# The sort of a graph kernel's edges: a 16-bit select whose sum lies in PSUM, a later release of GpSimd's spread, and fewer, longer relus on ScalarE

## Chip, cores and metric

One core of a Trainium2 chip. The metric is the device time of one execution in microseconds (us), lower is better.

## What is computed

A graph of N = 12,500 nodes with 64 features each and E = 412,500 directed edges (`src`, `dst`) with 4 attributes per edge passes two layers:

```
h = relu(layernorm(x));  x = x + L0(h, edges)      # hyperbolic attention layer: gather, edge weight, segment sum by source
h = relu(layernorm(x));  x = x + L1(h, edges, attr)  # message passing: gather, two products with batch norm, segment sum, two more
```

Both layers gather rows by the edge's two ends and sum over the edges of one source node. For both the kernel first sorts the edges by the chunk of 128 nodes to which their source belongs. The change lies in this sort alone, and the sort computes nothing but an order: each edge becomes a record (source within its chunk, destination, 4 attributes) in a table `rec_d`, where the records of one chunk stand together.

## The kernel before, in words

The program is written out by hand as phases with a barrier of all engines between them: a first norm and product, the sort (its supertiles run from about 315 us to about 2,880 us), the gathers and sums of the two layers, and the node updates. Within a phase every engine has its own instruction list in program order, and the engines hold each other by semaphores. There are no queues or planners that reorder anything.

The sort runs over NS = 124 supertiles. One supertile has J = 26 edges in each of 128 partitions (3,328 edges). NC = 99 is the number of chunks with a spare one. What one supertile s needs, engine by engine (lines are those of the kernel before):

- **VectorE, `flags` (L619):** one 0/1 row of 99 for each edge, equal to 1 at its chunk, in bfloat16 (`B3`, 2,574 elements for each partition, two buffers). It is done one supertile ahead, inside `supertile(s-1)`.
- **TensorE, `ranks` (L736 to L742):** 65 products with these rows (13 + 13 + 13 + 26) give the counts by chunk in PSUM (`RT`). At the end it signals `rt_rdy`.
- **VectorE, `supertile` (L654 to L697):** waits for `rt_rdy`; turns counts into starts (`INC`, L657), adds both (`A2`, two rows of 99, in PSUM, L658); selects for each of the 26 edges its own entry of `A2` by a product with the flags (L664, into `prod`, 2,574 float32) and a sum over 99 (L668, into `sel`); then a few operations on 26 elements split the position into a segment and a place in it (L669 to L675); L679 makes a one-hot of the place (`OHL`). After `seg_rdy` ScalarE may start. Then come the flags of s+1 (L619), 10 of the 26 segment one-hots of 512 columns (L686, `DH`), `before` for s+1 (L627 to L633), and the destinations (L691 to L697).
- **ScalarE, `segments` (L786, L792):** the other ACTD = 16 one-hots, as relu(1 - (iota - segment)^2): 16 squares, then 16 relus in place, each over one segment of 512, and at the end `da_rdy`.
- **GpSimd, `spread` (L835, L837):** multiplies the edges' 15 values by `OHL`, 624 and 2,496 elements, into `EX`. It reads `OHL` of s, but waits for `l_rdy`, which VectorE gives inside `supertile(s+1)`, between L658 and L664. At its end it gives `e_rdy`. Ahead of it stand `attributes` (L818 to L827), behind it four indirect DMAs (`scatter`, L849) for s-1.
- **TensorE, `place` (L752, L754):** waits for `e_rdy`, `d_rdy` and `da_rdy`; four passes of 27 products put the values into the places. At the end it gives `y_rdy`. TensorE's loop is `place(s)`, then `ranks(s+2)`.
- **VectorE, `take_out` (L641 to L645):** the last part of `supertile(s+1)` waits for `y_rdy` and copies the result of s out of PSUM.

So the release of the spread of s and the counts that `supertile(s+2)` starts with are tied together by TensorE's order:

```
    place(b)      # waits for e_rdy of s: the spread, released by l_rdy inside supertile(s+1)
    ranks(b)      # gives rt_rdy, for which supertile(s+2) waits at L654
```

Of the kernel before, what the change touches and what calls it, by code (L numbers as in the profile page):

```python
# [8 lines left out]
BF16 = mybir.dt.bfloat16  # L9
I32 = mybir.dt.int32  # L10
U16 = mybir.dt.uint16
ALU = mybir.AluOpType
ACT = mybir.ActivationFunctionType
AX = mybir.AxisListType.X
# [2 lines left out]
P = 128  # L17
# [32 lines left out]
def build(nc, x, src, dst, attr, w0t, wm1, bm1, gm1, betm1, wm2, bm2, gm2, betm2,  # L50
# [14 lines left out]
    with ctx:  # L65
# [341 lines left out]
        late_at = top[0]  # L407
        EX = [take(J * CH * L // 2, BF16) for _ in range(2)]
        EX4 = [e.rearrange("p (j c l) -> p j c l", c=CH, l=L) for e in EX]
        JNC = J * NC // 2  # L410
        B = [HA[:, 3 * COLS + b * JNC:3 * COLS + (b + 1) * JNC].bitcast(BF16) for b in range(2)]
        assert 3 * COLS + 2 * JNC <= NC * (D + AGW)
        B3 = [x.rearrange("p (j c) -> p j c", c=NC) for x in B]
        prod = take(J * NC)
        late_end = top[0]
        attb = [take(J * 4) for _ in range(2)]
        rem = take(J * 4)
# [4 lines left out]
        earlier_f = take(GJ * GJ)  # L422
        earlier = take(GJ * GJ // 2 + 1, BF16)[:, 0:GJ * GJ]
        wp = [take(J) for _ in range(2)]
        sel, seg_f = take(J), [take(J) for _ in range(2)]
        q_i, sg_i, l_i = (take(J, I32) for _ in range(3))
        stage = [take(NW * L * REC) for _ in range(2)]
        stage4 = [z.rearrange("p (w l c) -> p w l c", l=L, c=REC) for z in stage]
        ix = [take(NW, I32) for _ in range(2)]
        ACTD = 16  # L430
        iota_w = take(WS // 2, BF16)
        crow = take(NW * CH * L // 2, BF16)
        crow4 = crow.rearrange("p (w c l) -> p w c l", c=CH, l=L)
# [38 lines left out]
        RT = [ps[:, b * 512:b * 512 + 384] for b in range(2)]  # L472
        Y = [ps[:, 1024 + b * 512:1024 + b * 512 + NW * CH * L] for b in range(2)]
        Y4 = [y.rearrange("p (w c l) -> p w c l", c=CH, l=L) for y in Y]
        A2 = ps[:, 2048:2048 + 2 * NC].rearrange("p (g c) -> p g c", g=2)
        l_f = ps[:, 2560:2560 + J]
        zps = ps[:, 2560 + J:2561 + J].to_broadcast([P, NC])

        s_v, s_cntd, s_mm, s_pool, s_ld, s_bl, s_clr, h_rdy, h_used, s_hist, s_cast = (
# [12 lines left out]
        with nc.Block() as block:  # L492
# [37 lines left out]
            def _(v):  # L530
# [50 lines left out]
                for c, value in enumerate((-1.0, float(N // P * P), float(N % P))):  # L581
                    v.memset(crow4[0:1, :, c, :], value)
                v.memset(ANC[:, 0:1], 0.0)
                v.memset(ps[:, 2560 + J:2561 + J], 0.0)
                v.memset(ANC[:, NC + 1:NC + 2], float(DUMP + MID))
                link(v.memset(INC[:, 0:1], float(-MID)))
# [22 lines left out]
                def need(n):  # L609
                    v.wait_ge(s_c, n)  # L610
# [5 lines left out]

                def flags(b, s):

                    n = go(v.tensor_tensor(B3[b], iota_b[:, 0:NC].unsqueeze(1).to_broadcast([P, J, NC]),  # L619
                                           S[:, ds(s * J, J)].unsqueeze(2).to_broadcast([P, J, NC]), ALU.is_equal))  # L620
                    need(n)
                    v.sem_inc(b_rdy, 1)

# [27 lines left out]
                def supertile(b, s, first=False, last=False):  # L651
                    consume(v, rt_rdy)
                    n_all = RT[b][:, 256:256 + NC]
                    need(go(v.tensor_scalar(n_i, n_all, float(L - 1), None, ALU.add)))  # L654
                    need(go(v.tensor_scalar(n_i, n_i, 3, 3, ALU.logical_shift_right, ALU.logical_shift_left)))
                    need(go(v.tensor_copy(n8, n_i)))
                    need(go(v.tensor_tensor_scan(INC[:, 1:NC + 1], n8, zps, float(-MID), ALU.add, ALU.add)))  # L657
                    a2 = go(v.tensor_tensor(A2, INC[:, 0:NC].unsqueeze(1).to_broadcast([P, 2, NC]),  # L658
                                            RT[b][:, 0:256].rearrange("p (g c) -> p g c", g=2)[:, :, 0:NC], ALU.add))
                    go(v.tensor_tensor(gpos[1 - b], gpos[b], n_all, ALU.add))  # L660
                    need(a2)
                    if not first:
                        v.sem_inc(l_rdy, 1)
                    n = go(v.tensor_tensor(prod.rearrange("p (g j c) -> p g j c", g=2, j=GJ),  # L664
                                           B[b].rearrange("p (g j c) -> p g j c", g=2, j=GJ),
                                           A2.unsqueeze(2).to_broadcast([P, 2, GJ, NC]), ALU.mult))
                    need(n)
                    need(go(v.tensor_reduce(sel, prod.rearrange("p (j c) -> p j c", c=NC), AX, ALU.add)))  # L668
                    need(go(v.tensor_tensor(q_i, sel, wp[b], ALU.add)))  # L669
                    sg = go(v.tensor_scalar(sg_i, q_i, 3, None, ALU.arith_shift_right))  # L670
                    li = go(v.tensor_scalar(l_i, q_i, L - 1, None, ALU.bitwise_and))
                    need(sg)
                    seg = go(v.tensor_copy(seg_f[b], sg_i))
                    need(li)
                    lf = go(v.tensor_copy(l_f, l_i))  # L675
                    need(seg)
                    v.sem_inc(seg_rdy, 1)
                    need(lf)
                    need(go(v.tensor_tensor(OHL[b], iota_b[:, 0:L].unsqueeze(1).to_broadcast([P, J, L]),  # L679
                                            l_f.unsqueeze(2).to_broadcast([P, J, L]), ALU.is_equal)))  # L680
                    if not last:
                        flags(1 - b, s + 1)
                    if first:
                        v.wait_ge(s_cast, 5)
                    for j in range(J - ACTD):
                        n = go(v.tensor_scalar(DH[b][:, j * WS:(j + 1) * WS], iota_w, seg_f[b][:, j:j + 1], None, ALU.is_equal))  # L686
                    need(n)
                    v.sem_inc(d_rdy, 1)
                    if not last:
                        before(1 - b, s + 1)  # L690
                    need(go(v.tensor_tensor(ANC[:, 1:NC + 1], gpos[b], INC[:, 0:NC], ALU.subtract)))  # L691
                    need(go(v.tensor_tensor(STEP, ANC[:, 1:NC + 2], ANC[:, 0:NC + 1], ALU.subtract)))
                    for w in range(NW):
                        n = go(v.scalar_tensor_tensor(out=hit3[:, w, :], in0=INC, scalar=g8[:, w:w + 1], in1=STEP,
                                                      op0=ALU.is_le, op1=ALU.mult, accum_out=dsum[:, w:w + 1]))
                    need(n)
                    go(v.tensor_tensor(dest[b], dsum, g8, ALU.add))  # L697
                    if not first:
                        take_out(1 - b)
                    settle()  # L700
# [17 lines left out]
            def _(t):  # L718
# [14 lines left out]
                def ranks(b):  # L733
                    consume(t, b_rdy)
                    for j in range(GJ):
                        t.matmul(RT[b][:, 0:NC], tri_b, B3[b][:, j, :], start=(j == 0), stop=(j == GJ - 1))  # L736
                    for j in range(GJ, J):
                        t.matmul(RT[b][:, 128:128 + NC], tri_b, B3[b][:, j, :], start=(j == GJ), stop=False)
                    for j in range(GJ):
                        t.matmul(RT[b][:, 128:128 + NC], ones_b, B3[b][:, j, :], start=False, stop=(j == GJ - 1))  # L740
                    for j in range(J):
                        m = t.matmul(RT[b][:, 256:256 + NC], ones_b, B3[b][:, j, :], start=(j == 0), stop=(j == J - 1))  # L742
                    m.then_inc(rt_rdy, 1)

                def place(b):
# [21 lines left out]
            @block.scalar  # L767
            def _(a):
                a.wait_ge(s_v, 1)
                a.activation(Hd, I0, ACT.Copy).then_inc(s_cast, 1)  # L770
                a.wait_ge(s_v, 4)
                a.activation(S, I0, ACT.Copy).then_inc(s_cast, 1)
                a.wait_ge(s_hist, 1)
                a.wait_ge(s_v, 8)
                a.activation(PC[:, :, 0], I0, ACT.Copy, bias=1.0).then_inc(s_cast, 1)
                a.activation(PC[:, :, 1], I1, ACT.Copy, scale=-1.0).then_inc(s_cast, 1)
                a.activation(PC[:, :, 2], s_i, ACT.Copy, scale=-1.0).then_inc(s_cast, 1)

                a.wait_ge(s_cast, 5)

                def segments(b):
                    consume(a, seg_rdy)
                    consume(a, da_free[b])
                    for n in range(ACTD):
                        j = J - ACTD + n
                        a.activation(DH[b][:, j * WS:(j + 1) * WS], iota_w, ACT.Square, scale=-1.0,  # L786
                                     bias=seg_f[b][:, j:j + 1]).then_inc(s_sq, 1)
                    for n in range(ACTD):
                        j = J - ACTD + n
                        a.wait_ge(s_sq, n + 1)  # L790
                        o = DH[b][:, j * WS:(j + 1) * WS]
                        last = a.activation(o, o, ACT.Relu, scale=-1.0, bias=1.0)  # L792
                    last.then_inc(da_rdy, 1)
                    a.sem_inc(s_sq, -ACTD)
                with a.Fori(0, NS // 2) as i:
                    for b in range(2):
                        segments(b)
# [1476 lines left out]
```

## Time and profile before

| | |
|---|---|
| runs shown | 14502.01 us median of 3 (14497.61 to 14504.36) |
| the profiled execution's own time | 14510.89 us, its span 14509.2 us |
| sort, steady part: starts of L664 in the last 120 supertiles | 404.6 to 2837.8 us |
| busy over the span | PE 6055.6, VectorE 8188.4, ScalarE 4342.2, GpSimd 9916.9 us |

The busy times are sums over phases of quite different kinds: in the slices of the sort VectorE and ScalarE are busy nearly all the time, in the gather phases GpSimd alone is. Since the change touches the sort only, its stretch is what is to be read, and there one period from a supertile to the next. In a timeline, the number in brackets is the engine's idle time just before the row and what ended it; `DVEq`, `POOLq` and `ACTq` are the engines' own sequencers, which is how a wait on a semaphore shows.

### The profile page before, as it was taken

To read this page: it belongs to the slowest core of one execution; us is meant where nothing else is said; L and a number is where in the kernel's file an instruction comes from. 1 tells how busy PE (TensorE), PEld (TensorE's weight loads), DVE (VectorE), ACT (ScalarE), POOL (GpSimd) and SP (SyncE) were. 2 spreads that over 40 slices of the span, in tenths; PEclk is the share of its full clock that TensorE was granted. 3 is DMA by queue.
4 is the path that set the end of the run, shared out by engine and by line. 5 is a ranking of instruction groups with operands and counts; after the bars stand their busy time and mean duration, and the time that the engine had idled before them with its cause. 6 is when DMAs were issued, how large, how long until landed. Compare 5 with 4: busy or idle time off the path is not lost. (4 is left out here: it accounts for less than half of the span.)

```text
span 14509.2 us, 190139 instructions
## 1 busy us (share of the span) xinstructions
PE 6055.6 (42%) x50077; PEld 5002.8 (34%) x50078; DVE 8188.4 (56%) x17598; ACT 4342.2 (30%) x8364; POOL 9916.9 (68%) x10589
## 2 busy tenths in 40 slices
PE   3555555511111111111179633333333333388998
PEld 3554555511111111101178522222222222236997
DVE  6999999743343334334388844444444444467776
ACT  1888888800000000000078500000000000054334
POOL 0666666677777777777767467777777777704774
PEclk6777777755555555555599866666666666699999
DMA  2000000033333333333344322222222222274332
GB/s 68 9 9 9 9 9 9 17 92 88 88 87 88 88 88 86 88 84 91 81 129 151 93 77 81 81 81 81 81 81 82 81 81 81 79 249 132 106 106 77
DMA packets 1142542, 1160.65 MB, mean 80 GB/s; under 512 B 688977, under 2 KB 832977, under 8 KB 1142226
## 3 DMA queue, kind: packets, MB, share of 16 engines
q1 hardware_dynamic: 845842, 680.39, 16.7%
q0 software_dynamic: 235008, 248.13, 8.6%
q10 hardware_dynamic: 61632, 231.44, 4.1%
q8 instruction: 24, 0.39, 0.0%
q14 instruction: 36, 0.29, 0.0%
HBM read 872.56 MB, written 286.75 MB: 80 GB/s over the span
## 5 line engine op out<-in xcount | busy, mean ns | idle before, releaser
L1611 POOL DMA_INDIRECT big<-b_d,big x3424 | 3276.2, 957 | 1223.1 <-issue 978.0
L1097 POOL DMA_INDIRECT big<-h_d,big x3424 | 3308.0, 966 | 1054.6 <-issue 989.9
L1151 PE MATMUL ps<-big 128*128 x3424 | 653.3, 371 | 3687.2 <-PEq L148 3685.0
L1151 PEld LDWEIGHTS ps<-big 128*128 128x128 bf16 x3424 | 500.8, 164 | 3839.5 <-issue 3839.5
L1685 PE MATMUL ps<-big 128*128 x3424 | 566.3, 317 | 2845.9 <-PEq L148 2845.9
L1182 DVE TENSOR_TENSOR HA<-big 128x1024 f32<-128x1024 f32 x214 | 262.2, 1225 | 2559.4 <-DVEq L148 2558.4
L1685 PEld LDWEIGHTS ps<-big 128*128 128x128 bf16 x3424 | 410.1, 156 | 3164.8 <-issue 3164.7
L1934 POOL TENSOR_SCALAR big<-iota_f,big 128x128 f32<-128x128 f32 x1498 | 877.7, 609 | 814.5 <-DMA big<-rec_d 499.7
L1724 DVE TENSOR_TENSOR big<-ps,big 128x1024 f32<-128x1024 f32 x214 | 262.1, 1225 | 2057.6 <-DVEq L148 2057.6
L786 ACT ACTIVATE big<-big 128x512 bf16<-128x512 bf16 x1984 | 1228.9, 708 | 280.7 <-ACTq L148 280.7
L1105 ACT ACTIVATE big<-big 128x16 int32<-128x16 f32 x214 | 49.3, 230 | 4203.2 <-ACTq L148 4179.1
L792 ACT ACTIVATE big<-big 128x512 bf16<-128x512 bf16 x1984 | 1042.3, 614 | 0.0
L849 POOL DMA_INDIRECT rec_d<-big x496 | 839.3, 1692 | 282.1 <-POOLq L148 154.0
L1620 ACT ACTIVATE big<-big 128x16 int32<-128x16 f32 x214 | 49.1, 229 | 3104.5 <-ACTq L148 3104.5
L754 PE MATMUL ps<-big 128*128 128x120 bf16 x12896 | 976.5, 252 | 0.0
L754 PEld LDWEIGHTS ps<-big 128*128 128x128 bf16 x12896 | 952.1, 119 | 0.0
L1317 POOL TENSOR_SCALAR big<-iota_f,big 128x128 f32<-128x128 f32 x856 | 687.1, 818 | 265.4 <-DMA big<-rec_d 233.5
L1392 PE MATMUL ps<-big 128*128 128x128 f32 x6848 | 816.3, 277 | 102.2 <-DVE big L1317 89.3
L1392 PEld LDWEIGHTS ps<-big 128*128 128x128 f32 x6848 | 783.1, 192 | 135.2 <-issue 133.3
L1728 DVE TENSOR_REDUCE ps<-ps 128x256 f32<-128x768 f32 x856 | 820.5, 959 | 0.0
L2010 PE MATMUL ps<-big 128*128 128x64 f32 x6848 | 788.4, 273 | 1.0 <-DVE big L1934 0.9
L2010 PEld LDWEIGHTS ps<-big 128*128 128x128 f32 x6848 | 781.9, 192 | 1.2 <-issue 1.2
(407 smaller groups left out, 14633.5 us busy)
## 6 DMA issues: line engine op xcount, KB each, us to landing
big<-e_d SPq DMA_DIRECT2D x428, 512.0 KB, 3.2
rows_d<-big ACTq DMA_DIRECT2D x214, 544.0 KB, 2.8
big<-rows_d SPq DMA_DIRECT2D x214, 544.0 KB, 3.3
HA<-slots_d SPq DMA_DIRECT2D x214, 512.0 KB
big<-slots_d SPq DMA_DIRECT2D x214, 512.0 KB
e_d<-big ACTq DMA_DIRECT2D x214, 512.0 KB
big<-rec_d SPq DMA_DIRECT2D x860, 64.0 KB, 3.0
big<-h_d,big POOLq DMA_INDIRECT x3424
```

The source lines that it names most:

```text
L754: m = t.matmul(o, DH[b][:, j * WS + w * P:j * WS + (w + 1) * P], EX[b][:, j * CH * L:(j + 1) * CH * L], start=False, stop=(j == J - 1))
L786: a.activation(DH[b][:, j * WS:(j + 1) * WS], iota_w, ACT.Square, scale=-1.0, bias=seg_f[b][:, j:j + 1]).then_inc(s_sq, 1)
L792: last = a.activation(o, o, ACT.Relu, scale=-1.0, bias=1.0)
L849: gp.indirect_dma_start(rec_d, bass.IndirectOffsetOnAxis(ix[b][:, w:w + 1], 0), stage[b][:, w * L * REC:(w + 1) * L * REC], None).then_inc ...
L1097: gp.indirect_dma_start(G[g][:, t * ROW:(t + 1) * ROW], None, h0_d, bass.IndirectOffsetOnAxis(idx[g][:, t:t + 1], 0)).then_inc(gath[g], 16)
L1151: m = t.matmul(XS[h][:, n, 0:3 * D + 3], OT3[g % 2][:, o, :], T0[:, ds(chunks[o // 2] * TW, 3 * D + 3)], start=True, stop=True)
L1392: m = t.matmul(ps[:, o:o + P], O4[g][:, n * P:(n + 1) * P], G0[g][:, n * ROW:n * ROW + P], start=(n % 2 == 0), stop=(n % 2 == 1))
L1611: gp.indirect_dma_start(G[g][:, t * D:(t + 1) * D], None, b_d, bass.IndirectOffsetOnAxis(idx[g % 2][:, t:t + 1], 0)).then_inc(gath[g], 16)
L1685: m = t.matmul(XST[q % 2][:, n // 2, n % 2, :], OT3[g % 2][:, o, :], T1[:, ds(chunks[o // 2] * (3 * D), 3 * D)], start=True, stop=True)
L1728: v.tensor_reduce(x, XSQ[q % 2], AX, ALU.add).then_inc(s_e, 1)
L1934: last = eng.tensor_scalar(u1.O[b][:, n * P:(n + 1) * P], iota_f[:, :], u1.rec[b][:, n * REC:n * REC + 1], None, ALU.is_equal)
L2010: m = t.matmul(ps[:, o:o + D], u1.O[b][:, n * P:(n + 1) * P], MSG[b][:, n * D:(n + 1) * D], start=(n % 2 == 0), stop=(n % 2 == 1))
```

## The change

1. The chunk rows are one column longer, NCP = NC + 1 = 100 (`flags` writes 2,600 elements; the products in `ranks` still read 99 of each 100).
2. `A2` moves from PSUM to SBUF and is int16; `prod` is int16 too. So the select's product (L664) has two inputs in SBUF, all of 2 bytes.
3. A new addition folds the second 50 columns of `prod` onto the first 50 (1,300 elements, in place), and the reduce (L668) runs over 50 columns for each edge.
4. Its sum `sel` is in PSUM, no longer in SBUF.
5. `l_rdy` is given behind the new addition, no longer ahead of the product.
6. ACTD is 17: ScalarE makes 17 of the 26 one-hots, VectorE 9. The 17 relus become two, over 9 and 8 segments.

```diff
-        JNC = J * NC // 2
+        NCP = NC + 1
+        assert NCP % 4 == 0
+        JNC = J * NCP // 2
-        prod = take(J * NC)
+        prod = take(J * NCP // 2, I16)
+        prod3 = prod.rearrange("p (j c) -> p j c", c=NCP)
+        take(J * NC - J * NCP // 2)
-        sel, seg_f = take(J), [take(J) for _ in range(2)]
+        seg_f = [take(J) for _ in range(2)]
-        ACTD = 16
+        ACTD = 17
+        HALF = (ACTD + 1) // 2
-        A2 = ps[:, 2048:2048 + 2 * NC].rearrange("p (g c) -> p g c", g=2)
+        A2f = take(NCP, I16)
+        A2 = A2f.rearrange("p (g c) -> p g c", g=2)
+        sel = ps[:, 2624:2624 + J]
...
                     need(a2)
+                    n = go(v.tensor_tensor(prod.rearrange("p (g j c) -> p g j c", g=2, j=GJ),
+                                           B[b].rearrange("p (g j c) -> p g j c", g=2, j=GJ),
+                                           A2.unsqueeze(2).to_broadcast([P, 2, GJ, NCP]), ALU.mult))
+                    need(n)
+                    need(go(v.tensor_tensor(prod3[:, :, 0:NCP // 2], prod3[:, :, 0:NCP // 2],
+                                            prod3[:, :, NCP // 2:NCP], ALU.add)))
                     if not first:
                         v.sem_inc(l_rdy, 1)
-                    n = go(v.tensor_tensor(prod.rearrange("p (g j c) -> p g j c", g=2, j=GJ),
-                                           B[b].rearrange("p (g j c) -> p g j c", g=2, j=GJ),
-                                           A2.unsqueeze(2).to_broadcast([P, 2, GJ, NC]), ALU.mult))
-                    need(n)
-                    need(go(v.tensor_reduce(sel, prod.rearrange("p (j c) -> p j c", c=NC), AX, ALU.add)))
+                    need(go(v.tensor_reduce(sel, prod3[:, :, 0:NCP // 2], AX, ALU.add)))
...
-                    for n in range(ACTD):
-                        j = J - ACTD + n
-                        a.wait_ge(s_sq, n + 1)
-                        o = DH[b][:, j * WS:(j + 1) * WS]
+                    for n, m in ((0, HALF), (HALF, ACTD)):
+                        a.wait_ge(s_sq, m)
+                        o = DH[b][:, (J - ACTD + n) * WS:(J - ACTD + m) * WS]
                         last = a.activation(o, o, ACT.Relu, scale=-1.0, bias=1.0)
```

VectorE inside `supertile(s+1)`, from the sum `A2` to the first segment one-hot. Before:

```order
L658 TENSOR_TENSOR ps<-big,ps 128x198 [waits so_chain]
L660 TENSOR_TENSOR big<-big,ps 128x99
L664 TENSOR_TENSOR big<-HA,ps 128x2574 [waits so_chain]
L668 TENSOR_REDUCE big<-big 128x26 [waits so_chain]
L669 TENSOR_TENSOR big<-big 128x26 [waits so_chain]
L670 TENSOR_SCALAR big<-big 128x26 [waits so_chain]
L671 TENSOR_SCALAR big<-big 128x26
L673 CAST big<-big 128x26 [waits so_chain]
L675 CAST ps<-big 128x26 [waits so_chain]
L679 TENSOR_TENSOR big<-iota_b,ps 128x208 [waits so_chain]
L619 TENSOR_TENSOR HA<-iota_b,HA 128x2574 [waits so_chain]
```

Of the change (its line numbers are higher by 9 to 11):

```order
L667 TENSOR_TENSOR big<-big,ps 128x2x99 [waits so_chain]
L669 TENSOR_TENSOR big<-big,ps 128x99
L671 TENSOR_TENSOR big<-HA,big 128x2600 [waits so_chain]
L675 TENSOR_TENSOR big<-big 128x26x50 [waits so_chain]
L679 TENSOR_REDUCE ps<-big 128x26 [waits so_chain]
L680 TENSOR_TENSOR big<-ps,big 128x26 [waits so_chain]
L681 TENSOR_SCALAR big<-big 128x26 [waits so_chain]
L682 TENSOR_SCALAR big<-big 128x26
L684 CAST big<-big 128x26 [waits so_chain]
L686 CAST ps<-big 128x26 [waits so_chain]
L690 TENSOR_TENSOR big<-iota_b,ps 128x208 [waits so_chain]
L628 TENSOR_TENSOR HA<-iota_b,HA 128x2600 [waits so_chain]
```

One operation has come in between the product and the reduce (L675 of the changed kernel). `l_rdy` is given behind it, where it was given ahead of the product. The reduce now writes PSUM, and the operation behind it reads PSUM.

ScalarE's part of one supertile, in the changed kernel:

```order
L797 ACTIVATE big<-big 128x512 [waits so_seg,so_dafree1]
L797 ACTIVATE big<-big 128x512 x16
L802 ACTIVATE big<-big 128x4608 [waits so_square]
L802 ACTIVATE big<-big 128x4096 [waits so_square]
```

Two relus stand where 16 were, and there are 17 squares (L797).

## Rows read from the trace of the kernel before

**Rows 1.** Line L664 as a source, 400 to 2850 us: duration min/median/max, first and last start
```profile
L664 DVE TENSOR_TENSOR big<-HA,ps x120: 2835/2835/2837, 404.6 to 2837.8; 128x2574 f32<-128x2574 bf16 x120
```

**Rows 2.** Who waited for whom, 400 to 2850 us: total us, times, longest us
```profile
ACT big L786 <- ACTq L148: 267.3, 120, 2.4
```

**Rows 3.** Timeline of one supertile: start us, us, engine, line, operation, [idle before]
```profile
1999.89 2.84 DVE L664 TENSOR_TENSOR big<-HA,ps 128x2574 f32<-128x2574 bf16 x1
2000.18 1.24 POOL L835 TENSOR_TENSOR big<-HA,big 128x624 bf16<-128x624 bf16 x1 [3.89 <-POOLq L148]
2001.38 4.40 POOL L837 TENSOR_TENSOR big<-big 128x2496 bf16<-128x2496 bf16 x1
...
2005.86 0.18 DVE L670 TENSOR_SCALAR big<-big 128x26 int32<-128x26 int32 x1
...
2006.33 0.11 PEld L752 LDWEIGHTS ps<-big 128*128 128x128 bf16 x1 [9.89 <-issue]
...
2006.95 2.84 DVE L619 TENSOR_TENSOR HA<-iota_b,HA 128x2574 bf16<-128x2574 bf16 x1 [0.18 <-DVE big L679]
2007.01 3.69 POOL L849 DMA_INDIRECT rec_d<-big  x1 [1.23 <-POOLq L148]
...
2012.60 1.53 PE L754 MATMUL ps<-big 128*128 128x120 bf16 x26
...
2015.77 1.37 PE L742 MATMUL ps<-HA,big 128*128 128x99 bf16 x26
...
2018.50 0.26 DVE L654 TENSOR_SCALAR big<-ps 128x99 int32<-128x99 f32 x1 [0.46 <-DVEq L148]
...
2020.20 2.83 DVE L664 TENSOR_TENSOR big<-HA,ps 128x2574 f32<-128x2574 bf16 x1
```

**Rows 4.** Stretches: length, busy us (and count) by engine, PEclk granted, DMA share, GB/s
```profile
2006.40:2008.40 2.00, 2.00 (x21) 2.00 (x22) 1.82 (x2) 1.88 (x4) 1.39 (x1) 0.50 0.00 0
...
2012.60:2017.10 4.50, 4.50 (x95) 4.38 (x91) 4.02 (x16) 4.50 (x9) 3.63 (x7) 1.00 0.07 19
```

**Rows 5.** Groups of the sort by line: total us, mean ns
```profile
L786 ACT ACTIVATE big<-big 128x512 bf16<-128x512 bf16 x1984 | 1228.9, 708 | 280.7 <-ACTq L148 280.7
L792 ACT ACTIVATE big<-big 128x512 bf16<-128x512 bf16 x1984 | 1042.3, 614 | 0.0
...
L686 DVE TENSOR_SCALAR big<-big 128x512 bf16<-128x512 bf16 x1240 | 416.1, 406 | 18.9 <-DVE HA L619 9.3
...
L668 DVE TENSOR_REDUCE big<-big 128x26 f32<-128x2574 f32 x124 | 351.3, 2833 | 4.3
...
L633 DVE TENSOR_REDUCE big<-big 128x26 f32<-128x338 bf16 x124 | 62.7, 505 | 4.3
L627 DVE TENSOR_TENSOR big<-HA 128x338 bf16 x120 | 61.3, 511 | 18.0 <-DVE big L686 9.0
...
L631 DVE TENSOR_TENSOR big<-big 128x338 bf16<-128x338 bf16 x124 | 41.7, 336 | 4.3
...
L655 DVE TENSOR_SCALAR big<-big 128x99 int32<-128x99 int32 x124 | 26.3, 212 | 4.4
...
L670 DVE TENSOR_SCALAR big<-big 128x26 int32<-128x26 int32 x124 | 22.1, 178 | 4.3
```

**Rows 6.** Timeline of the second supertile, where VectorE and GpSimd meet
```profile
349.84 0.27 POOL L818 CAST big<-big 128x104 bf16<-128x104 f32 x1 [0.34 <-POOLq L148]
349.88 0.26 DVE L673 CAST big<-big 128x26 f32<-128x26 int32 x1
...
350.69 2.84 DVE L619 TENSOR_TENSOR HA<-iota_b,HA 128x2574 bf16<-128x2574 bf16 x1
350.73 2.93 POOL L823 CAST big<-big 128x104 bf16<-128x104 f32 x1 [0.17 <-POOL big L820]
```

**Rows 7.** Timeline of the first supertile: the end of the ranks, VectorE's next
```profile
321.67 2.37 PE L742 MATMUL ps<-HA,big 128*128 128x99 bf16 x26
...
324.19 0.26 DVE L654 TENSOR_SCALAR big<-ps 128x99 int32<-128x99 f32 x1 [4.36 <-DVEq L148]
```

More of the change, by code:

```diff
@@ L11 @@
 U16 = mybir.dt.uint16
+I16 = mybir.dt.int16
 ALU = mybir.AluOpType
@@ L409, in build @@
         EX4 = [e.rearrange("p (j c l) -> p j c l", c=CH, l=L) for e in EX]
-        JNC = J * NC // 2
+        NCP = NC + 1
+        assert NCP % 4 == 0
+        JNC = J * NCP // 2
         B = [HA[:, 3 * COLS + b * JNC:3 * COLS + (b + 1) * JNC].bitcast(BF16) for b in range(2)]
         assert 3 * COLS + 2 * JNC <= NC * (D + AGW)
-        B3 = [x.rearrange("p (j c) -> p j c", c=NC) for x in B]
-        prod = take(J * NC)
+        B3 = [x.rearrange("p (j c) -> p j c", c=NCP) for x in B]
+        prod = take(J * NCP // 2, I16)
+        prod3 = prod.rearrange("p (j c) -> p j c", c=NCP)
+        take(J * NC - J * NCP // 2)
         late_end = top[0]
@@ L583, in _ @@
                 v.memset(ANC[:, 0:1], 0.0)
+                v.memset(A2f, 0.0)
                 v.memset(ps[:, 2560 + J:2561 + J], 0.0)
@@ L617, in flags @@
                 def flags(b, s):
-                    n = go(v.tensor_tensor(B3[b], iota_b[:, 0:NC].unsqueeze(1).to_broadcast([P, J, NC]),
-                                           S[:, ds(s * J, J)].unsqueeze(2).to_broadcast([P, J, NC]), ALU.is_equal))
+                    n = go(v.tensor_tensor(B3[b], iota_b[:, 0:NCP].unsqueeze(1).to_broadcast([P, J, NCP]),
+                                           S[:, ds(s * J, J)].unsqueeze(2).to_broadcast([P, J, NCP]), ALU.is_equal))
                     need(n)
@@ L657, in supertile @@
                     need(go(v.tensor_tensor_scan(INC[:, 1:NC + 1], n8, zps, float(-MID), ALU.add, ALU.add)))
-                    a2 = go(v.tensor_tensor(A2, INC[:, 0:NC].unsqueeze(1).to_broadcast([P, 2, NC]),
+                    a2 = go(v.tensor_tensor(A2[:, :, 0:NC], INC[:, 0:NC].unsqueeze(1).to_broadcast([P, 2, NC]),
                                             RT[b][:, 0:256].rearrange("p (g c) -> p g c", g=2)[:, :, 0:NC], ALU.add))
@@ L735, in ranks @@
                     for j in range(GJ):
-                        t.matmul(RT[b][:, 0:NC], tri_b, B3[b][:, j, :], start=(j == 0), stop=(j == GJ - 1))
+                        t.matmul(RT[b][:, 0:NC], tri_b, B3[b][:, j, 0:NC], start=(j == 0), stop=(j == GJ - 1))
                     for j in range(GJ, J):
-                        t.matmul(RT[b][:, 128:128 + NC], tri_b, B3[b][:, j, :], start=(j == GJ), stop=False)
+                        t.matmul(RT[b][:, 128:128 + NC], tri_b, B3[b][:, j, 0:NC], start=(j == GJ), stop=False)
                     for j in range(GJ):
-                        t.matmul(RT[b][:, 128:128 + NC], ones_b, B3[b][:, j, :], start=False, stop=(j == GJ - 1))
+                        t.matmul(RT[b][:, 128:128 + NC], ones_b, B3[b][:, j, 0:NC], start=False, stop=(j == GJ - 1))
                     for j in range(J):
-                        m = t.matmul(RT[b][:, 256:256 + NC], ones_b, B3[b][:, j, :], start=(j == 0), stop=(j == J - 1))
+                        m = t.matmul(RT[b][:, 256:256 + NC], ones_b, B3[b][:, j, 0:NC], start=(j == 0), stop=(j == J - 1))
                     m.then_inc(rt_rdy, 1)
```

## Prediction

> **What bounds the kernel now.** The change lies in the sort alone, so I read one period of the sort, not the page's shares. First the product L664 as a source: between its first and last start lie 119 supertiles, (2837.8 - 404.6) / 119 = **20.45 us a period** [rows 1]. Then who waits: ScalarE stands before its squares for 267.3 / 120 = 2.2 us a supertile [rows 2]. In the timeline of one supertile GpSimd stood idle for 3.89 us before its spread, TensorE for 9.89 us before its placement, VectorE for only 0.46 us before L654 [rows 3], mostly the handling of semaphores. So VectorE sets the period.
>
> The timeline [rows 3] shows a second loop that doesn't bind yet. The spread starts 0.29 us after L664 does, when `l_rdy` is given (1999.89 to 2000.18), and lasts 5.60 us (to 2001.38 + 4.40 = 2005.78). The placement starts 0.55 us later (2006.33), and placement and the ranks behind it end at 2015.77 + 1.37 = 2017.14, which is 10.81 us. Only then can the supertile after next pass L654. In the first supertile, where VectorE really waited, L654 came 0.15 us after the last rank (321.67 + 2.37 = 324.04 to 324.19) [rows 7]. From L654 to L664 are 1.70 us. Sum: 0.29 + 5.60 + 0.55 + 10.81 + 0.15 + 1.70 = 19.10 us from one L664 to the next. Against 20.45 that is a slack of 1.35 us, **and the change puts its new delay of `l_rdy` into this loop**.
>
> **The change, part by part.**
>
> *The select.* L631 and L627 both have 338 elements of 2 bytes; L631 (a product, in place) takes 336 ns, L627 (one input repeats each element) 511 [rows 5]. L668 and L633, reduces of 2,574 and 338 elements, give (2833 - 505) / 2236 = 1.04 ns an element and 153 ns fixed. So L627 runs at one element a step, 1.04 ns, L631 at two, 0.52 ns with 160 ns fixed. The new product has 2-byte operands that run along rows of 100 as L631's do: 2,600 x 0.52 + 160 = 1.51 us in place of 2.84. The new addition: 1,300 x 0.52 + 160 = 0.84 us. The reduce, 1,300 elements: 1,300 x 1.04 + 153 = 1.51 us in place of 2.83. With a step of 0.03 us behind each of the first two, `l_rdy` comes at 2.42 us after the product's start, where it came at 0. No row has a product of bfloat16 with int16. Its bounds are L631's rate (1.51 us) and L664's own (2.84 us at 2,574 elements, 2.87 at 2,600); I take the first, since L631 is nearest in width and layout. The operands in PSUM (`sel`, its reader) change operations of 26 elements, bounded by their 0.2 us rows: nothing.
>
> *VectorE's own sum.* Before, L664 to L670 took 2005.86 - 1999.89 = 5.97 us [rows 3]. Now the same way is 2.42 + 1.51 + 0.03 for the reduce, 0.24 for the operation behind it = 4.20 us, 1.77 less. One one-hot fewer: L686 has a mean of 0.41 us, ten of them overlapped in about 3.4, so 0.34 less. The flags have 26 elements more: 0.03 us. If nothing else held VectorE, its period would be 20.45 - 2.08 = 18.37 us.
>
> *ScalarE.* 16 squares keep it busy for 1228.9 / 124 = 9.91 us, 16 relus for 1042.3 / 124 = 8.41 [rows 5]. 17 squares: 10.53 us. The relus over 17 segments cost 8.93 us at most, at the old price by segment, less with two long ones; the engine thus needs no more than 19.5 us. Under a period of over 21 us this is hidden in either case; it would cost something only if the period came under 19.5.
>
> *The release.* The loop above grows by 2.42: 19.10 + 2.42 = **21.52 us**. That alone is 1.07 us above today's period. The spread gets no shorter by the change, nor do placement and ranks (99 columns each as before).
>
> *What the spread now meets on VectorE.* This is the larger term. Two pairs of rows [rows 6] show that the engines hold each other. VectorE's L619 (two inputs in SBUF) ran from 350.69 to 353.53; a GpSimd cast that began at 350.73 and should take 0.27 us took 2.93, till 353.66. And it goes the other way too: GpSimd's L818 held 349.84 to 350.11, VectorE's L673 began at 349.88 and ended at 350.14, 0.26 us in place of 0.18. GpSimd's L849, which began 0.06 us after L619, needed 3.69 us [rows 3]. Before the change the spread (2000.18 to 2005.78) lay beside L664 and L668 alone, which have one input in SBUF each, and both engines ran undisturbed; it ended 0.08 us before L670. Now it starts at 2.42 + 0.29 = 2.71 us behind the product's start and ends at 8.31, while VectorE comes to L670 at 4.20. L670 is one of the kind of L673: 26 elements of 4 bytes, SBUF to SBUF. L655 and L670, the same operation on 99 and 26 elements, take 212 and 178 ns [rows 5], 0.47 ns an element, half of 1.04, so this kind reads two elements a step and can be expected to need what GpSimd holds. L837 takes over from L835 at 3.91, before L670 is there. I take it that L670 waits for the end of L837, as L673 did for L818; the nearest row is that one, with a wait of hundredths. Its start is then as if at 8.31 + 0.10 - 0.18 = 8.23 us, where it was at 5.97: **2.26 us later**. Less 0.34, plus 0.03, the period is 20.45 + 1.95 = **22.40 us**. The bounds: no wait at all, and the loop of 21.52 us binds; a wait as taken, 22.40.
>
> The Trainium skill says in "SBUF — State Buffer", section "Who interferes with whom", that a VectorE instruction in a mode with two ports, or with two SBUF inputs while GpSimd reads SBUF, and a GpSimd instruction exclude each other for the whole instruction, and that whoever issues first wins. By that rule L670 waits to the end of L837, 4.1 us, which is the 22.40; without it the sum would be 21.52. The 2.93 us of L823 agree with it; that VectorE stands behind a GpSimd instruction of 4.4 us no row here shows.
>
> *The wait that VectorE then carries.* Behind L670 stand its signal to ScalarE, the flags, the one-hots and `take_out`. ScalarE gets its segments at about 8.9 us in place of 6.6; it ends 18 to 19.5 us later, at 28.4 at most, while their placement starts at 22.40 + 8.86 = 31.3. Covered. The first scatter DMA still starts 1.23 us after the spread, beside the flags, which still begin about 1.1 us after it, so that meeting stays as it is. The ranks end at 8.86 + 10.81 = 19.67 and L654 is due at 22.40 - 1.70 = 20.70: the second loop has 0.9 us to spare.
>
> *Sum.* About 122 of the 124 supertiles run so (the first has no release; the second is not yet in step). 122 x 1.95 = 238 us. The profiled execution took 14510.89 us, so 14749; it stands 8.9 above the median of 14502, so **14740**. The rest of the program isn't touched.
>
> **The rivals.**
>
> *No wait at L670, or only at the flags* (17%). Short operations may not be held, and L619, which has two inputs in SBUF and would be due at 5.3, then waits until 8.31. From L619 to the next L664 are 2020.20 - 2006.95 = 13.25 us [rows 3], 12.94 with one one-hot fewer, so VectorE's loop is 21.3 us and the one through TensorE binds at 21.52: 122 x 1.07 = 131 us, **14633**. For it: the held rows are few. Against it: L673's stretched row.
>
> *The product runs at one element a step* (8%), since its types are mixed. Then `l_rdy` comes 1.36 us later still, and both loops with it: 122 x 3.31 = 404 us, **14905**. For it: no row has such a product. Against: all three tensors are 2 bytes wide.
>
> *The scatter gets ahead of the flags* (5%): the first L849 and L619 are due within 0.2 us of each other. Before, L849 had 3.69 - (2006.95 + 2.84 - 2007.01) = 0.91 us left when L619 was through, its own work. If it comes first and holds VectorE for these 0.91 us, the period is that much longer: 14740 + 122 x 0.91 = **14851**.
>
> *Faster* (7%): TensorE leaves the lower of its clock levels earlier, and L670 isn't held. The placement starts at a granted clock of 0.50, 1.2 GHz, after 9.89 us of idleness, and its last pass and the ranks run at 1.00, 2.4 GHz [rows 4]. From the placement's start to its last pass are 2012.60 - 2006.33 = 6.27 us; at that pass's pace [rows 3] 3 x 1.53 = 4.59, 1.68 less. The loop would be 19.84 us, 0.61 under today's: **14428**. It decides from where placement and ranks together fall from 10.81 below 9.74 us. Against it: TensorE's idle time gets longer with the period, and it has to start each placement from idleness as before. VectorE's 18.37 us alone, 122 x 2.08 = 254 us gained (14248), can't be reached while the spread's loop stands.
>
> *No change* (3%): the same mechanism, half way.
>
> **How the numbers follow.** The likeliest case, L670 held, has 60%: 14740. A measurement of this kernel tells about 0.2%, 29 us, from no change. Slower by more than that are all cases but the last two: 60 + 17 + 8 + 5 = 90%; within it 3%; faster 7%. The range leaves out the product at one element a step and the faster cases, 18%: from 14620, a little under the loop of 21.52 us, to 14855, above the scatter's case.
>
> **What the changed profile would show.** The period of the select's product 22.4 us; the product near 1.51, the addition 0.84, the reduce 1.51 us; the first operation on 26 int32 elements at 4.2 us mean in place of 0.18, ending with GpSimd's L837; L837 still at 4.40; GpSimd's scatter unchanged; ScalarE's wait before the squares up from 2.2 to about 4 us. The forecast is wrong if that operation stays at 0.18 us: then the flags are stretched or L654 waits for TensorE, and the period is 21.5. A product of 2.87 us would be the second rival. A period under 20.4 needs placement and ranks under 9.7 us.

## The result and the profile after

The changed kernel takes 14728.56 us (median of 4, 14727.46 to 14735.67), the kernel before 14502.05 us in the same comparison: ratio 1.0158, 95% interval 1.0145 to 1.0171. It is slower by 226.5 us, where 238 were forecast (14740, range 14620 to 14855).

The select's product as a source, in the profile of the changed kernel, answers to [rows 1]:

```profile
L671 DVE TENSOR_TENSOR big<-HA,big x120: 1502/1504/1507, 405.3 to 3059.5; 128x2600 int16<-128x2600 bf16 x120
```

(3059.5 - 405.3) / 119 = **22.30 us a period**, where it was 20.45, so 1.86 us more; 22.40 was forecast. 226.5 / 1.86 = 122 supertiles, so the whole loss lies here. The product takes 1504 ns, as forecast (1.51 us): bfloat16 times int16 runs at two elements a step like L631.

The waits of the steady part; ScalarE's answers to [rows 2]:

```profile
POOL big L845 <- POOLq L149: 714.5, 117, 6.4
ACT big L797 <- ACTq L149: 503.9, 116, 4.6
...
DVE big L663 <- DVEq L149: 74.0, 117, 0.8
```

ScalarE stands 503.9 / 116 = 4.3 us before its squares (2.2 before), GpSimd 6.1 us before its spread. VectorE stands 74.0 / 117 = 0.6 us at L663, which waits for the ranks, and stood 0.6 us at the same place before (75.0 us in 120 times at L654): the loop through TensorE doesn't bind.

The timeline of one supertile, which answers to [rows 3]:

```profile
2011.55 1.50 DVE L671 TENSOR_TENSOR big<-HA,big 128x2600 int16<-128x2600 bf16 x1
2013.09 0.84 DVE L675 TENSOR_TENSOR big<-big 128x1300 int16<-128x1300 int16 x1
2014.07 1.51 DVE L679 TENSOR_REDUCE ps<-big 128x26 f32<-128x1300 int16 x1
2014.37 1.24 POOL L845 TENSOR_TENSOR big<-HA,big 128x624 bf16<-128x624 bf16 x1 [6.34 <-POOLq L149]
2015.57 4.40 POOL L847 TENSOR_TENSOR big<-big 128x2496 bf16<-128x2496 bf16 x1
2015.62 0.18 DVE L680 TENSOR_TENSOR big<-ps,big 128x26 int32<-128x26 f32 x1
2015.84 4.16 DVE L681 TENSOR_SCALAR big<-big 128x26 int32<-128x26 int32 x1
2019.92 0.17 DVE L682 TENSOR_SCALAR big<-big 128x26 int32<-128x26 int32 x1
...
2020.51 0.10 PEld L763 LDWEIGHTS ps<-big 128*128 128x128 bf16 x1 [11.48 <-issue]
...
2020.92 2.87 DVE L628 TENSOR_TENSOR HA<-iota_b,HA 128x2600 bf16<-128x2600 bf16 x1 [0.18 <-DVE big L690]
2021.19 3.50 POOL L859 DMA_INDIRECT rec_d<-big  x1 [1.23 <-POOLq L149]
...
2023.94 2.91 DVE L697 TENSOR_SCALAR big<-big 128x512 bf16<-128x512 bf16 x9 [0.16 <-DVE HA L628]
...
2030.91 7.54 ACT L802 ACTIVATE big<-big 128x4608 bf16<-128x4608 bf16 x2
...
2032.08 0.26 DVE L663 TENSOR_SCALAR big<-ps 128x99 int32<-128x99 f32 x1 [0.47 <-DVEq L149]
...
2033.71 1.50 DVE L671 TENSOR_TENSOR big<-HA,big 128x2600 int16<-128x2600 bf16 x1
```

The product begins at 2011.55, the addition takes 0.84 us, and release and reduce come at 2014.07; GpSimd's spread begins 0.30 us later and ends at 2015.57 + 4.40 = 2019.97. The first shift on 26 elements, L681, has 0.18 us of work; it begins at 2015.84 and ends at 2020.00. Two other signs stand in the same lines: L847 kept its 4.40 us, so it was VectorE that waited, and the next operation, L682, is back at 0.17 us. The flags (L628) begin 0.92 us after the end of L681, and the DMA instruction L859, which starts beside them, takes 3.50 us, where it took 3.69. The wait is no accident of one supertile; L681 as a source, min/median/max:

```profile
L681 DVE TENSOR_SCALAR big<-big x120: 4158/4161/4169, 409.6 to 3063.8; 128x26 int32<-128x26 int32 x120
```

The groups of the sort on ScalarE, and VectorE's one-hots, against [rows 5]:

```profile
L797 ACT ACTIVATE big<-big 128x512 bf16<-128x512 bf16 x2108 | 1304.7, 707 | 537.8 <-ACTq L149 537.8
...
L802 ACT ACTIVATE big<-big 128x4608 bf16<-128x4608 bf16 x124 | 499.4, 4028 | 0.0
L802 ACT ACTIVATE big<-big 128x4096 bf16<-128x4096 bf16 x124 | 446.5, 3601 | 0.0
L697 DVE TENSOR_SCALAR big<-big 128x512 bf16<-128x512 bf16 x1116 | 359.8, 393 | 18.9 <-DVE HA L628 9.3
```

The two relus take 4.03 and 3.60 us where 16 took 8.41; 17 squares and two relus are 10.53 + 7.53 = 18.1 us, which is hidden.

### The profile page after: what moved, and what is told of

Same layout as the page of the kernel before. It is cut to its first block and busy times, and to the rows that moved or that the text cites. A ratio compares the mean times of both kernels' runs of the same rounds, so it can differ in the third digit from the quotient of the medians.

```text
span 14734.0 us, 188528 instructions
## 1 busy us (share of the span) xinstructions
PE 6030.3 (41%) x50077; PEld 4977.4 (34%) x50078; DVE 8398.2 (57%) x17599; ACT 4310.2 (29%) x6752; POOL 9847.4 (67%) x10589
## 5 line engine op out<-in xcount | busy, mean ns | idle before, releaser
L797 ACT ACTIVATE big<-big 128x512 bf16<-128x512 bf16 x2108 | 1304.7, 707 | 537.8 <-ACTq L149 537.8
L859 POOL DMA_INDIRECT rec_d<-big x496 | 779.9, 1572 | 283.4 <-POOLq L149 155.1
L802 ACT ACTIVATE big<-big 128x4608 bf16<-128x4608 bf16 x248 | 934.2, 3814 | 0.0
```

What stands on the lines that cost most here:

```text
L859: gp.indirect_dma_start(rec_d, bass.IndirectOffsetOnAxis(ix[b][:, w:w + 1], 0), stage[b][:, w * L * REC:(w + 1) * L * REC], None).then_inc ...
```

## The experiments

**Take the small operations off GpSimd's path** (`x1_small_in_psum`). Positions, segments and places move to PSUM, so no shift or cast goes from SBUF to SBUF:

```diff
-        q_i, sg_i, l_i = (take(J, I32) for _ in range(3))
+        take(3 * J)
+        q_i, sg_i, l_i = (ps[:, 2688 + n * 32:2688 + n * 32 + J].bitcast(I32) for n in range(3))
```

> The changed kernel with q_i, sg_i and l_i in PSUM, so that the shifts and casts on 26 elements no longer go from SBUF to SBUF. Theory A (these operations need what GpSimd holds during its spread, and the wait of 4.16 us at the first of them sets the period of 22.31 us): they take about 0.2 us again, the flags, which have two inputs in SBUF, are then the ones that wait, till the spread's end; VectorE's loop falls to 21.3 us and the loop through the spread, placement and ranks binds at 21.5: 14728 - 122 x 0.8 = about 14630 us. Theory B (the wait only fills a gap; the late release alone, through TensorE, costs the time): no change, 14728.

Measured: 14654.74 us (ratio to before 1.0102, 1.0085 to 1.0119). Its product as a source gives (2979.0 - 406.0) / 119 = 21.62 us a period:

```profile
L672 DVE TENSOR_TENSOR big<-HA,big x120: 1502/1505/1508, 406.0 to 2979.0; 128x2600 int16<-128x2600 bf16 x120
```

Its timeline, GpSimd's second multiplication, the first shift, the flags:

```profile
2010.06 4.40 POOL L848 TENSOR_TENSOR big<-big 128x2496 bf16<-128x2496 bf16 x1
...
2010.33 0.19 DVE L682 TENSOR_SCALAR ps<-ps 128x26 int32<-128x26 int32 x1
...
2011.45 5.72 DVE L629 TENSOR_TENSOR HA<-iota_b,HA 128x2600 bf16<-128x2600 bf16 x1 [0.18 <-DVE big L691]
```

The shift takes 0.19 us beside the running spread. The flags, with two inputs in SBUF, begin at 2011.45 and end at 2017.17, 5.72 us for 2.87 us of work: they started while L848 ran and got through 2.7 us after its end at 2014.46. So theory A holds in both halves, and B, by which nothing would change, falls. A wait of 4.0 us is gone and one of 2.85 has come in its place. The stretched flags aren't alone in setting this period: in 78 of 117 supertiles of the steady part L664 starts less than 0.2 us after the last rank, so it waited for TensorE; in the change that is so in 11 of 117.

**Take the flags off it as well** (`x2_flags_too`):

```diff
+        iota_q = ps[:, 2944:2944 + NCP]
+                v.tensor_copy(iota_q, iota_f[:, 0:NCP])
-                    n = go(v.tensor_tensor(B3[b], iota_b[:, 0:NCP].unsqueeze(1).to_broadcast([P, J, NCP]),
+                    n = go(v.tensor_tensor(B3[b], iota_q.unsqueeze(1).to_broadcast([P, J, NCP]),
```

> As x1, and the flags read their row of numbers from PSUM, so nothing on VectorE meets the spread. Theory A with the second loop (spread, placement and ranks come behind the release, and the supertile after next waits for the ranks): VectorE would need 18.4 us a period, but now waits for TensorE at the first operation of the supertile, about 3 us each; period 21.5, about 14630 us, the same as x1. Rival C (there is no such second loop that matters): period 18.4 us, 14728 - 122 x 3.9 = about 14250.

Measured: 14659.6 us (1.0104, 1.0087 to 1.0121), the same as x1. No operation of VectorE is stretched, yet nothing is gained. Its waits and four rows of its timeline say where the time is:

```profile
DVE big L653 <- DVEq L149: 375.4, 121, 5.4
DVE big L666 <- DVEq L149: 212.9, 120, 1.8
```

```profile
2014.63 2.46 DVE L700 TENSOR_SCALAR big<-big 128x512 bf16<-128x512 bf16 x9 [0.16 <-DVE HA L631]
...
2024.33 0.17 DVE L653 CAST big<-big 128x4 int32<-128x4 f32 x1 [3.85 <-DVEq L149]
...
2025.47 1.33 PE L756 MATMUL ps<-HA,big 128*128 128x99 bf16 x26
...
2026.96 0.26 DVE L666 TENSOR_SCALAR big<-ps 128x99 int32<-128x99 f32 x1 [1.77 <-DVEq L149]
```

VectorE stands (375.4 / 121) + (212.9 / 120) = 4.9 us a supertile, first for the placement's result (L653, `take_out`), then for the ranks (L666). About 0.9 us of that stands in the change too, so the loop adds 4.0, where about 3 were expected; nine one-hots in 2.46 us, 2.91 in the change, are part of the difference. The last rank ends at 2025.47 + 1.33 = 2026.80 and L666 starts 0.16 us later; over 117 supertiles that distance is never more than 0.2 us. This is the second loop, and rival C (14250) is out. Its sum had been 21.52; x1 and x2 give 21.6. Both loops are thus real, 22.3 us through VectorE's wait and 21.6 through TensorE, and taking the first away only uncovers the second. Of the 1.86 us that the change loses in each period, the wait at L681 accounts for 0.7 alone; 1.2 stay without it, because the release is late.

**Put the release back ahead of the product** (`x3_release_first`):

```diff
+                    if not first:
+                        v.sem_inc(l_rdy, 1)
                     n = go(v.tensor_tensor(prod.rearrange(...), ALU.mult))
...
-                    if not first:
-                        v.sem_inc(l_rdy, 1)
```

> The changed kernel with the release put back ahead of the product. Theory A (whoever comes first holds the other off for a whole instruction): the product starts first and takes 1.5 us, GpSimd's first multiplication waits for it; then the addition has to wait for GpSimd. If GpSimd's two instructions follow each other without a gap for VectorE, the addition ends near 7.9 us and the reduce comes after it: period 23.7, about 14900 us. If the addition slips in between them, the period is about 22.0, 14690. Theory B (only the release matters for the time): the release is 2.4 us earlier, period 20.45 or below, at most 14502.

Measured: 14638.82 us (1.009, 1.0073 to 1.0107), 90 us faster than the change, and slower than before; neither of A's sums is met, B's is missed by 137. The timeline of this kernel shows how the engines take turns:

```profile
2018.66 1.51 DVE L673 TENSOR_TENSOR big<-HA,big 128x2600 int16<-128x2600 bf16 x1
2018.96 2.31 POOL L845 TENSOR_TENSOR big<-HA,big 128x624 bf16<-128x624 bf16 x1 [3.57 <-POOLq L149]
2020.21 1.76 DVE L677 TENSOR_TENSOR big<-big 128x1300 int16<-128x1300 int16 x1
2021.24 4.99 POOL L847 TENSOR_TENSOR big<-big 128x2496 bf16<-128x2496 bf16 x1
2022.00 1.52 DVE L679 TENSOR_REDUCE ps<-big 128x26 f32<-128x1300 int16 x1
...
2023.77 2.49 DVE L681 TENSOR_SCALAR big<-big 128x26 int32<-128x26 int32 x1
```

The product came first; L845 needed 2.31 us for 1.24. Then the addition, ready at 2020.21, had its turn when L845 ended, 1.76 us for 0.84. L847 needed 4.99 for 4.40 and ended at 2026.23, L681 at 2026.26. So the spread ends 7.57 us behind the product's start, against 8.42 in the change: its two waits cost GpSimd 1.07 + 0.59 = 1.7 us and the early release gives 2.5 (0.30 us behind the product in place of 2.82). Between two GpSimd instructions that follow each other directly a waiting VectorE instruction does get in, which the slip case of the expectation had; its size was off, 22.0 us a period for (2965.6 - 405.6) / 119 = 21.51. That this kernel beats the change says that behind the addition isn't the best place for the release.

**The late release alone, in the kernel before** (`x6_late_release_only`):

```diff
-                    if not first:
-                        v.sem_inc(l_rdy, 1)
                     n = go(v.tensor_tensor(prod.rearrange(...), ALU.mult))
                     need(n)
+                    if not first:
+                        v.sem_inc(l_rdy, 1)
```

> The kernel before with one thing changed: the release is given behind the product, 2.87 us later; product, reduce and everything else are as before. Theory A: the spread ends at 2.87 + 0.29 + 5.60 = 8.76 us behind the product's start, the first shift is due at 5.97 and waits 2.7 us: period 23.1 us, 14502 + 122 x 2.7 = about 14830. Theory B (the loop through TensorE alone): 19.10 + 2.87 = 21.97 us, 14502 + 122 x 1.5 = about 14690.

Measured: 14864.71 us (1.0246, 1.0229 to 1.0263). The product as a source gives (3192.5 - 414.0) / 119 = 23.35 us a period:

```profile
L662 DVE TENSOR_TENSOR big<-HA,ps x120: 2826/2828/2830, 414.0 to 3192.5; 128x2574 f32<-128x2574 bf16 x120
```

And the operation that now waits, beside GpSimd's second multiplication and over all supertiles:

```profile
2006.41 4.40 POOL L837 TENSOR_TENSOR big<-big 128x2496 bf16<-128x2496 bf16 x1
2007.78 3.07 DVE L669 TENSOR_TENSOR big<-big 128x26 int32<-128x26 f32 x1
```

```profile
L669 DVE TENSOR_TENSOR big<-big x120: 3065/3070/3075, 419.8 to 3198.3; 128x26 int32<-128x26 f32 x120
```

It isn't the shift L670 here but L669 ahead of it, which in this kernel adds two operands in SBUF: 3.07 us for 0.20, to 2010.85, where L837 ends at 2010.81. In the change the sum that it reads is in PSUM, and it took 0.18 beside the running spread. The place of the release alone, with no 16-bit select, costs 2.9 us a period, a little more than the 2.7 expected; theory B, with 14690 us, is out.

**ScalarE's part alone** (`x4_scalare_only`), in the kernel before:

```diff
-        ACTD = 16
+        ACTD = 17
+        HALF = (ACTD + 1) // 2
...
-                    for n in range(ACTD):
-                        j = J - ACTD + n
-                        a.wait_ge(s_sq, n + 1)
-                        o = DH[b][:, j * WS:(j + 1) * WS]
+                    for n, m in ((0, HALF), (HALF, ACTD)):
+                        a.wait_ge(s_sq, m)
+                        o = DH[b][:, (J - ACTD + n) * WS:(J - ACTD + m) * WS]
```

> The kernel before with the ScalarE part of the change alone: 17 of 26 one-hots there, relus over 9 and 8 segments. VectorE has one operation less of 0.34 us and it sets the period; ScalarE needs about 18.1 us. Period 20.45 - 0.34 = 20.11: 14502 - 41 = about 14461 us. Rival (ScalarE's half matters by itself): no change, or slower if ScalarE's longer work reached the placement, which it doesn't by the rows.

Measured: 14456.92 us (0.9971, 0.9961 to 0.9982) against 14499.37 for before in this comparison, 42 us faster. Period (2788.6 - 401.2) / 119 = 20.06 us:

```profile
L665 DVE TENSOR_TENSOR big<-HA,ps x120: 2835/2837/2837, 401.2 to 2788.6; 128x2574 f32<-128x2574 bf16 x120
```

With 18 on ScalarE (`x4b_scalare18`), the same edit and `ACTD = 18`:

> As x4, with 18 of 26 one-hots on ScalarE, relus over 9 and 9 segments. VectorE 0.68 us less than before: period 19.77; ScalarE 18 x 0.62 + 2 x 4.0 = 19.2 us and a few tenths between two supertiles, just under it; the loop through TensorE 19.1. So 14502 - 122 x 0.68 = about 14420 us. If ScalarE or TensorE binds first, 14450.

Measured: 14415.61 us (0.9944, 0.993 to 0.9958), period (2745.0 - 401.8) / 119 = 19.69 us:

```profile
L665 DVE TENSOR_TENSOR big<-HA,ps x120: 2835/2837/2839, 401.8 to 2745.0; 128x2574 f32<-128x2574 bf16 x120
```

Both as expected. This part of the change is a gain of its own.

**The change without ScalarE's part** (`x5_without_scalare`), the edit above undone:

> The changed kernel with the ScalarE part taken back: 16 one-hots there with 16 relus. The one-hot that returns to VectorE stands behind the wait for the spread, so it lengthens the period by 0.34 us: 14728 + 41 = about 14770 us. If the period were set through TensorE it would cost nothing: 14728.

Measured: 14795.51 us (1.0206, 1.0192 to 1.022), 67 us over the change. Period (3122.2 - 408.0) / 119 = 22.81 us, 0.50 more:

```profile
L670 DVE TENSOR_TENSOR big<-HA,big x120: 1503/1503/1507, 408.0 to 3122.2; 128x2600 int16<-128x2600 bf16 x120
```

Work behind the wait lengthens the period, so the wait sets it. The size, 0.50 for 0.34, was off. Most of it is to be seen in the traces of before and after: ten one-hots overlapped take 3.37 us in the one, nine take 2.91 in the other, so the tenth is worth about 0.45.

**Put the spread where VectorE needs nothing of what it holds** (`x7_spread_under_flags`). On top of x2:

```diff
-        n_i = take(NC, I32)
+        n_i = ps[:, 2816:2816 + NC].bitcast(I32)
...
                 def take_out(b):
...
-                    go(v.tensor_copy(ix[b], dest[b]))
+                    c = go(v.tensor_copy(ix[b], dest[b]))
+                    need(c)
+                    v.sem_inc(l_rdy, 1)
...
                     go(v.tensor_tensor(gpos[1 - b], gpos[b], n_all, ALU.add))
+                    if not last:
+                        flags(1 - b, s + 1)
                     need(a2)
...
-                    if not first:
-                        v.sem_inc(l_rdy, 1)
...
-                    if not last:
-                        flags(1 - b, s + 1)
```

At the end of the first supertile `l_rdy` is given without a `take_out`; the one behind the last supertile falls away.

> The changed select kept, but the spread of a supertile is released at the end of the same supertile, in take_out, behind its first cast; all that VectorE does until the spread's end reads PSUM or has one input: the shifts of the counts and of the positions go from PSUM, and the flags, with their row of numbers in PSUM, stand ahead of the product. The theory of the two loops gives: from the release to the product 0.8 + 0.5 + 1.6 + 2.9 = 5.8 us, as long as the spread's 5.9, so VectorE hardly waits and has its own 18.4 us; the loop through TensorE has 2 us to spare; ScalarE needs 18.1 and a few tenths. Period about 18.5 us: 14502 - 122 x 1.95 = about 14265 us. If some other meeting of the two engines holds VectorE as in the change, 14500 or more.

Measured: 14384.82 us (0.9923, 0.9909 to 0.9936). It is faster than both kernels (by all that it moves together; no run parts it), but the period is (2701.8 - 404.1) / 119 = 19.31 us, not 18.5:

```profile
L678 DVE TENSOR_TENSOR big<-HA,big x120: 1511/1512/4272, 404.1 to 2701.8; 128x2600 int16<-128x2600 bf16 x120
```

Its timeline:

```profile
2003.40 4.40 POOL L851 TENSOR_TENSOR big<-big 128x2496 bf16<-128x2496 bf16 x1
2003.62 0.27 DVE L668 TENSOR_SCALAR ps<-ps 128x99 int32<-128x99 f32 x1 [0.93 <-DVEq L149]
...
2005.42 7.53 ACT L806 ACTIVATE big<-big 128x4608 bf16<-128x4608 bf16 x2
...
2013.10 0.26 PE L767 MATMUL ps<-big 128*128 128x120 bf16 x1 [9.62 <-PEq L149]
...
2013.25 10.52 ACT L801 ACTIVATE big<-big 128x512 bf16<-128x512 bf16 x17 [0.30 <-ACTq L149]
...
2023.90 0.27 DVE L668 TENSOR_SCALAR ps<-ps 128x99 int32<-128x99 f32 x1 [1.53 <-DVEq L149]
```

The spread ends at 2003.40 + 4.40 = 2007.80 and no longer holds VectorE. But the placement begins at 2013.10, 0.15 us after ScalarE's second relu (2005.42 + 7.53 = 2012.95): the placement now waits for ScalarE, which I had only counted by its busy time. The loop goes over two supertiles: 18.3 us from ScalarE's release to the placement, 10.8 for placement and ranks, 0.15 to L668 of the supertile after next, and 9.6 from L668 (2003.62) to ScalarE's next start (2013.25): 38.9 us for two, 19.4 each. Two runs were made to test this reading.

**Ranks ahead of the placement** (`x8_ranks_first`), x7 with:

```diff
                     for b in range(2):
-                        place(b)
                         ranks(b)
+                        place(b)
```

> As x7, with TensorE's order turned: the ranks of s+2, whose flags are now made early, ahead of the placement of s. In x7 the placement waits for ScalarE, not for the spread: from its segments' release 18.3 us to the placement, 10.8 + 0.15 us of placement and ranks to the first operation of the supertile after next, and 9.6 us from there to the next release of that buffer, 38.9 us for two supertiles, 19.4 each (measured 19.3). If that is the loop, the ranks leave it (3.1 us for two supertiles less, and TensorE is at its upper clock level already when the placement begins), and VectorE's and ScalarE's own sums of about 18.5 us bind: 14502 - 122 x 1.9 = about 14270 us. If x7's remaining time has another cause, no change against x7, 14385, or slower, since the placement starts behind the ranks.

Measured: 14280.98 us (0.9853, 0.9837 to 0.987). The product as a source, here over all 124 supertiles, gives (2609.0 - 327.4) / 123 = 18.55 us a period:

```profile
L678 DVE TENSOR_TENSOR big<-HA,big x124: 1511/1511/4273, 327.4 to 2609.0; 128x2600 int16<-128x2600 bf16 x124
```

**One one-hot back from ScalarE** (`x9_x7_with16`), x7 with `ACTD = 16`:

> As x7, with 16 instead of 17 one-hots on ScalarE. By the loop over two supertiles ScalarE's part is 0.62 + 0.41 = 1.0 us shorter, so each period 0.5 us, although VectorE has one operation more: 19.3 - 0.5 = 18.8 us, 14385 - 122 x 0.5 = about 14325 us. If VectorE's sum bound in x7, it would be 0.3 to 0.5 us a period slower: about 14430.

Measured: 14319.32 us (0.9879, 0.9862 to 0.9895), period (2654.0 - 402.9) / 119 = 18.92 us, where 18.8 was expected. Less for ScalarE and more for VectorE is 65 us faster; VectorE's sum didn't bind in x7. Both runs came out as the loop over two supertiles says. x8 beats both kernels by far: 1.5% under before, 3.0% under the change.

## Why the prediction was right

- **What bounds.** VectorE's chain with 20.45 us a period, and a second loop of 19.10 us through spread, placement and ranks. x2 made the second one bind: 21.6 us measured, 19.10 + 2.42 = 21.52 forecast. The terms of that sum came from one supertile. Placement and ranks took 10.81 us there; over the steady part they vary from 10.1 to 11.7 us, with a mean of 11.0 before and 10.9 in x2, so a match within 0.1 us is in part luck.
- **The select.** 1.51, 0.84 and 1.51 us forecast, 1.50, 0.84 and 1.52 measured. The rival of one element a step is out.
- **The wait.** This carried the forecast, and was the one step that no row of before showed at its size: a stretch of 0.08 us was read as the sign of a wait of four. L681 takes 4.16 us and ends 0.03 us after the spread. x1 shows that it is the operation's own operands that make it wait, since in PSUM it takes 0.19 us at the same place; x5 and x1 together show that this wait sets the period. The rule of the Trainium skill ("SBUF — State Buffer", section "Who interferes with whom"), an exclusion for the whole instruction, agrees with L681 (4.16 us for 0.18), with the flags in x1 (5.72 for 2.87) and with L669 in x6 (3.07 for 0.20).
- **The first rival** (the flags wait in its place and the loop through TensorE binds, 14633) is what x1 made: 14655.
- **ScalarE's part.** Forecast as 0.34 us on VectorE and hidden otherwise. It is 0.39 alone (x4: 20.45 - 20.06) and 0.50 in the change (x5).
- **The sum.** From the product to the flags are 2020.92 - 2011.55 = 9.37 us, where they were 2006.95 - 1999.89 = 7.06: 2.31 more, 2.26 forecast. From the flags to the next product are 2033.71 - 2020.92 = 12.79 us, where they were 13.25: 0.46 less, 0.31 forecast, mostly because the tenth one-hot was worth 0.45 us and not 0.34, and because L663 to L671, between which no release is given any more, takes 1.63 us where L654 to L664 took 1.70. 22.40 + 0.05 - 0.15 = 22.30, the measured period, and 0.10 us in 122 supertiles are the 11 us by which the forecast was high. That the first difference is only 0.05 is luck: the spread started 2.82 us behind the product and not 2.71, and L681 ended 0.03 us behind the spread and not 0.10.
- **The scatter rival.** L859 began 0.27 us behind the flags (2021.19 against 2020.92), and the flags kept their 2.87 us, so it cost nothing.
- **Faster.** In the supertiles shown TensorE's idle time before the placement grew from 9.9 to 11.5 us, and its first pass took 2.8 us as before. This case needed placement and ranks under 9.74 us; over the steady part of the change they took 10.8 on average and never less than 10.0.

The expectations of x3 (by 50 us) and of x7 (by 120 us) failed on sizes and on a loop left out; in x7 I had weighed ScalarE by its busy time and not by who waits for its end.

## What to carry to other kernels

Before an operation is moved or a release is shifted, list for each engine what runs beside it afterwards, and for VectorE beside GpSimd which operands lie in SBUF: a shift of 0.18 us beside the wrong GpSimd instruction stood 4.0 us in every period, more than the 1.7 us that the faster select had gained up to that shift. A busy time says whether an engine is full, not whether it is in a loop; write down each loop with its number of iterations, because a gain on one only uncovers the next (22.3, 21.6, 19.3, 18.5 us here). And when two engines exclude each other, put beside the long instruction operations that it doesn't hold, here those with operands in PSUM, and don't delay the long instruction until the fast part is over: the operands in PSUM alone (x2) left the kernel slower than before, and only with the release moved as well (x7, x8) was it faster.

## What the runs showed of the hardware beyond what was expected

- The same addition on 26 elements took 3.07 us with both operands in SBUF (x6) and 0.18 with one of them in PSUM (the change), both beside a running GpSimd multiplication.
- A VectorE instruction that is already waiting gets in between two GpSimd instructions that follow each other directly (x3: addition between L845 and L847); one that comes after the second has begun waits for all of it (L681 in the change).
- VectorE's flags, 2,600 elements, take 2.87 us with the row of numbers as bfloat16 in SBUF and 2.87 or 2.86 with it as float32 in PSUM (x2, x7): moving it cost nothing.
